# Gathering x2 by source into the tile that uses it, and gathering h2 into a ring of four slots

## What is computed

```python
x = _layernorm(x + _L0(x, edge_attr_48, src, dst, eps))       # relu(x[src] + e) summed by dst
x = _layernorm(x + _L1(x, src, dst, W, b))                    # degree-weighted x[src] summed by dst, @ W
x = _layernorm(x + _L2(x, edge_index, W, b))                  # degree-weighted x[dst] summed by src, @ W
x = _layernorm(x + _L3(x, edge_index, edge_attr_40, ...))     # gated x[dst] summed by src, layernorm, gamma, beta
```

## Time and profile before

| what | value |
|---|---|
| median of the timed runs | 2671.04 us |
| span of the profiled execution | 3047.5 us |
| VectorE busy | 1926.7 us, 63% |
| GpSimd busy | 1858.8 us, 61%, 1768 instructions |
| ScalarE busy | 632.0 us, 21% |
| TensorE busy | 633.7 us, 21% |
| indirect DMAs in `ring`, per gather of 196 | 199.5 to 214.6 us busy |

### The profile page before, as it was taken

One profiled execution on the slowest core, in us unless ns is written; L12 is line 12 of the kernel. 1 busy time (PEld: TensorE's weight loads), 2 busy tenths in 40 slices (PEclk: granted clock), 3 DMA queues, 4 the chain that ended last, 5 costly groups with the idle time before them and its releaser, 6 DMA issues.

```text
span 3047.5 us, 12805 instructions
## 1 busy us (share of the span) xinstructions
PE 633.7 (21%) x2848; PEld 506.5 (17%) x2848; DVE 1926.7 (63%) x2735; ACT 632.0 (21%) x1121; POOL 1858.8 (61%) x1768
## 2 busy tenths in 40 slices
PE   1111600000028875554422100001430000000000
PEld 0000300000028765443422100001330000000000
DVE  2001799999717766754623825997349999948872
ACT  1001800222113332211211101322112223221110
POOL 4774002777766664556175757777556676574776
PEclk8555955555555555666555555555555555555555
DMA  3110086787014433322860193443122223110000
GB/s 118 22 22 13 1 323 231 257 322 269 16 34 142 142 125 103 86 53 55 49 46 13 18 71 114 130 137 119 50 59 72 87 69 103 58 41 9 17 16 15
DMA packets 158467, 276.20 MB, mean 91 GB/s; under 512 B 88601, under 2 KB 113507, under 8 KB 158259
## 3 DMA queue, kind: packets, MB, share of 16 engines
q1 hardware_dynamic: 96675, 206.39, 24.0%
q0 software_dynamic: 56448, 44.23, 8.7%
q10 hardware_dynamic: 5264, 24.74, 2.2%
HBM read 142.41 MB, written 138.17 MB: 92 GB/s over the span
## 4 chain that ended last, share of the span: by engine, by line
DVE 27%; POOL 22%; issue 16%; another core or an unknown queue 12%; PE 8%; DMA 8%; ACT 7%; SPq 0%; ACTq 0%; DVEq 0%; POOLq 0%
POOL XD L470 7%; POOL out L507 7%; POOL x_table L507 3%; POOL ring L457 3%; PE psT L883 2%; DMA din<-x_table 2%; DMA din<-in_xaux 2%; POOL x_with_degree L507 2%; DVE du L1345 2%; DVE var L1351 2%; DVE psS L1342 2%; DVE do L1362 2%; DMA xa_table<-din 2%; DVE sumb L1270 2%
## 5 line engine op out<-in xcount | busy, mean ns | idle before, releaser
L470 POOL DMA_INDIRECT XD<-xa_table,dstI x196 | 222.1, 1133 | 290.5 <-SPq L360 231.0
L507 POOL DMA_INDIRECT x_table<-sumb,put x196 | 212.6, 1085 | 154.7 <-ACT sumb L619 86.5
L457 POOL DMA_INDIRECT ring<-x_with_degree,srcI x196 | 208.2, 1062 | 146.0 <-DVEq L1426 85.1
L592 ACT ACTIVATE sq<-du 128x1344 f32<-128x1344 f32 x129 | 168.9, 1321 | 536.7 <-DVE du L1345 416.5
L457 POOL DMA_INDIRECT ring<-h_by_src,zs x196 | 214.6, 1095 | 104.0 <-issue 63.5
L457 POOL DMA_INDIRECT ring<-x_table,srcI x196 | 199.5, 1018 | 121.1 <-issue 63.2
L507 POOL DMA_INDIRECT x_with_degree<-sumb,put x196 | 209.6, 1070 | 94.0 <-issue 58.1
L507 POOL DMA_INDIRECT out<-sumb,put x196 | 201.9, 1030 | 94.9 <-issue 60.9
L457 POOL DMA_INDIRECT ring<-edge_records,dstI x196 | 202.2, 1032 | 86.8 <-issue 57.6
L470 POOL DMA_INDIRECT XD<-in_xaux,srcI x196 | 187.7, 958 | 87.9 <-issue 60.3
L1240 DVE TENSOR_SCALAR GX<-GX 128x784 bf16<-128x784 int16 x196 | 74.7, 426 | 253.3 <-remote 204.1
(11 more groups left out here) (322 smaller groups left out, 2907.4 us busy)
## 6 DMA issues: line engine op xcount, KB each, us to landing
din<-in_xaux SPq DMA_DIRECT2D x56, 728.0 KB
xa_table<-din SPq DMA_DIRECT2D x28, 728.0 KB
x_table<-GX SPq DMA_DIRECT2D x28, 686.0 KB
x_with_degree<-GX SPq DMA_DIRECT2D x28, 686.0 KB
din<-x_table SPq DMA_DIRECT2D x28, 686.0 KB
x_table<-do SPq DMA_DIRECT2D x28, 672.0 KB
din<-x_table SPq DMA_DIRECT2D x28, 672.0 KB
out<-do SPq DMA_DIRECT2D x28, 672.0 KB
```

Source lines behind the costliest of these rows:

```text
L457: pool.indirect_dma_start(ring[:, h, t, 0:w], None, table, bass.IndirectOffsetOnAxis(ap=of[:, c * H + t:c * H + t + 1], axis=0), **skip).t ...
L470: pool.indirect_dma_start(XD[:, t, 0:w], None, table, bass.IndirectOffsetOnAxis(ap=of[:, t:t + 1], axis=0)).then_inc(rows[c].sem, rows[c]. ...
L507: pool.indirect_dma_start(table, bass.IndirectOffsetOnAxis(ap=put[:, c * H + t:c * H + t + 1], axis=0), rows_of[:, h, t, :], None, bounds_ ...
L592: nc.scalar.activation(sq[:, h, :, :], u, ACT.Square).then_inc(S["squared"], 1)
```

## The change

The x2 gather goes straight to `XD`, column by column, with one semaphore for each turn (`rows_in[c]`), and needs no slot, no copy and no wait. VectorE waits for these semaphores instead of `kept`. The h2 gather uses the memory of `ring` as `ring4`, four slots of 14 x 48 words without gaps (2688 of 2772 words), with a semaphore for each slot's rows and one, `h2_free`, for free slots. ScalarE loads the first two record turns and refills all four slots before the h2 phase, and in the term stage refills the slot that term c has read for turn c + 4.

```diff
+        ring4 = ring[:, :, :, :].rearrange("p h c w -> p (h c w)")[:, 0:4 * H * D].rearrange(
+            "p (h c d) -> p h c d", h=4, d=D)
...
-            def gather_x2(of):
-
-                for c in range(2):
-                    ring_used(c)
-                    gather_turn(X2, D, of, c)
-                gather(X2, D, of, first=2)
+            def gather_h2(of):
+
+                filled, (h2_free,) = views("h2_fill0", "h2_fill1", "h2_fill2", "h2_fill3"), views("h2_free")
+                for c in range(CE // H):
+                    pool.wait_ge(h2_free.sem, h2_free.up())
+                    for t in range(H):
+                        pool.indirect_dma_start(
+                            ring4[:, c % 4, t, :], None, H2,
+                            bass.IndirectOffsetOnAxis(ap=of[:, c * H + t:c * H + t + 1], axis=0),
+                            bounds_check=last_edge, oob_is_err=False
+                                ).then_inc(filled[c % 4].sem, filled[c % 4].add())
...
-            gather_x2(srcI)
+            gather_in_place(X2, D, srcI)
             pool.wait_ge(S["h2_st"], 16 * NBLK)
-            gather(H2, D, put4, bounds_check=last_edge, oob_is_err=False)
+            gather_h2(put4)
...
-            def rows_of_src(c):
-                h = c % 2
-                act.wait_ge(fill[h].sem, fill[h].up(H))
-                nc.scalar.activation(XS[:, c * H:(c + 1) * H, :], ring[:, h, :, 0:D], ACT.Copy
+            def refill(h):
+                nc.scalar.activation(ring4[:, h, :, :], rows[:, 0, :].unsqueeze(1).broadcast_to([P, H, D]), ACT.Copy
                                      ).then_inc(own.sem, own.add())
                 act.wait_ge(own.sem, own.now())
-                if c >= CE // H - 2:
-                    refill(h)
-                act.sem_inc(S["ring_free"], 1)
-                act.sem_inc(S["kept"], 1)
...
-            KEPT_EARLY = {0: (0,), 1: (1,), 3: (2,), 4: (3,), 6: (4,)}
-            KEPT_LATE = {0: (5,), 1: (6,), 2: (7, 8), 3: (9, 10), 4: (11, 12), 5: (13,)}
             h2_rows = H2.rearrange("(p c) d -> p c d", p=P)
+            for h in range(2):
+                act.wait_ge(rb_st[h].sem, rb_st[h].now())
+                load_back(h, h)
+            for h in range(4):
+                refill(h)
+                act.sem_inc(S["h2_free"], 1)
             for i in range(NBLK):
                 evacuate()
                 cols = bass.ds(i * R, R)
                 act.wait_ge(h2_ready.sem, h2_ready.up())
                 act.dma_start(h2_rows[:, cols, :], M[:, cols, :]).then_inc(h2_st.sem, h2_st.add())
-                for c in KEPT_EARLY.get(i, ()):
-                    rows_of_src(c)
-            for h in range(2):
-                act.wait_ge(rb_st[h].sem, rb_st[h].now())
-                load_back(h, h)
...
             def terms_of(c, h, last=False):
                 act.wait_ge(ring_read.sem, ring_read.up())
-                refill(h)
-                act.sem_inc(S["ring_free"], 1)
-                unit = [(h, du[:, h, 0:H, :])]
+                if c + 4 < CE // H:
+                    refill(c % 4)
+                    act.sem_inc(S["h2_free"], 1)
...
-                dve.wait_ge(kept.sem, kept.up(2))
+                for c in (2 * i, 2 * i + 1):
+                    dve.wait_ge(rows_in[c].sem, rows_in[c].up(H))
...
-                dve.wait_ge(fill[h].sem, fill[h].up(H))
-                V.tensor_tensor(u, ring[:, h, :, 0:D], back[:, h, :, 0:D], ALU.add).then_inc(S["ring_read"], 1)
+                dve.wait_ge(filled[c % 4].sem, filled[c % 4].up(H))
+                V.tensor_tensor(u, ring4[:, c % 4, :, :], back[:, h, :, 0:D], ALU.add).then_inc(S["ring_read"], 1)
```

More of the change, by code:

```diff
@@ L251, in bass_gnn @@
             "rec_ready", "rec_st", "srt_ready", "srt_st", "srt_ld",
-            "rb_st0", "rb_st1", "rb_ld0", "rb_ld1", "ring_read", "h2_ready", "h2_st", "by_src", "w1c", "srt_in", "kept",
-            "zt_ready", "zt_st", "z_ld0", "z_ld1", "z_free") + ROWS}
+            "rb_st0", "rb_st1", "rb_ld0", "rb_ld1", "ring_read", "h2_ready", "h2_st", "by_src", "w1c", "srt_in",
+            "zt_ready", "zt_st", "z_ld0", "z_ld1", "z_free", "h2_fill0", "h2_fill1", "h2_fill2", "h2_fill3",
+            "h2_free") + ROWS}
         FROM_DMA = ("look", "g_ld", "g_fill", "g_st", "consts", "edges", "ea48", "xa_ld0", "xa_ld1", "ld0", "ld1",
                     "st0", "st1", "fill0", "fill1", "sc0", "sc1", "mlp_ld0", "mlp_ld1", "mlp_ld2", "mlp_ld3", "rec_st",
-                    "srt_st", "srt_ld", "rb_st0", "rb_st1", "rb_ld0", "rb_ld1", "h2_st", "srt_in", "zt_st", "z_ld0", "z_ld1") + ROWS
+                    "srt_st", "srt_ld", "rb_st0", "rb_st1", "rb_ld0", "rb_ld1", "h2_st", "srt_in", "zt_st", "z_ld0", "z_ld1",
+                    "h2_fill0", "h2_fill1", "h2_fill2", "h2_fill3") + ROWS
         def views(*names):
@@ L772, in _ @@
             function(t0[:, :])
-            def rows_of_src(c):
-                h = c % 2
-                act.wait_ge(fill[h].sem, fill[h].up(H))
-                nc.scalar.activation(XS[:, c * H:(c + 1) * H, :], ring[:, h, :, 0:D], ACT.Copy
-                                     ).then_inc(own.sem, own.add())
-                act.wait_ge(own.sem, own.now())
-                if c >= CE // H - 2:
-                    refill(h)
-                act.sem_inc(S["ring_free"], 1)
-                act.sem_inc(S["kept"], 1)
             def refill(h):
-                nc.scalar.activation(ring[:, h, :, 0:D], rows[:, 0, :].unsqueeze(1).broadcast_to([P, H, D]), ACT.Copy
+                nc.scalar.activation(ring4[:, h, :, :], rows[:, 0, :].unsqueeze(1).broadcast_to([P, H, D]), ACT.Copy
                                      ).then_inc(own.sem, own.add())
@@ L809, in _ @@
                     dense_pair()
-                for c in KEPT_LATE.get(i, ()):
-                    rows_of_src(c)
             act.wait_ge(h2_st.sem, h2_st.now())
@@ L1035, in _ @@
             ld, st, rows_in = views("ld0", "ld1"), views("st0", "st1"), views(*ROWS)
-            squared, std_ready, kept, mm, counted = views("squared", "std_ready", "kept", "mm", "counted")
+            squared, std_ready, mm, counted = views("squared", "std_ready", "mm", "counted")
             mm_used, spread, returned = views("mm_used", "spread", "returned")
@@ L1636, in _ @@
                     dense_pair()
-            rb_ld = views("rb_ld0", "rb_ld1")
+            rb_ld, filled = views("rb_ld0", "rb_ld1"), views("h2_fill0", "h2_fill1", "h2_fill2", "h2_fill3")
             def terms_of(c, h):
@@ L1656, in terms_of @@
                 summed(h, 2)
-            for h in range(2):
-                fill[h].n = 3 * CE // 2 * 16
             term_turn = {own: 8, fill[0]: H, fill[1]: H, spread: 4, ring_read: 2, squared: 2, std_ready: 2,
```

## The result

The changed kernel takes 2631.28 us, the median of 4 runs (2629.29 to 2637.12), beside 2671.36 us for the kernel before (4 runs, 2667.68 to 2671.83): ratio 0.9855, 95% interval 0.9839 to 0.9871, so 40.1 us less. The number of the forecast, 2632, holds. One step of its working does not, and it is the one on which everything else was scaled.

What follows compares the result with a forecast made beforehand. GpSimd's late h2 gather was taken to bound the last terms, once the stalls were put down to profiling. Small edits cost 0, so 2671.0 - 38.7 = 2632.3, forecast 2632 us, range 2622 to 2645.

Steps and rivals of the forecast that it cites:

- the stalls belong to the profiled execution: Whole kernel: 368.7 us of unknown-queue waits exist only in the profiled run; 3047.5 - 368.7 = 2678.8, against 2671.0 timed.
- what bounds the kernel now: Opening step: VectorE bounds the first four term pairs, 49.9 us each; from term 8 GpSimd's 19.84 us turns are late.
- R2: h2 phase: stalls beside a gather are real and grow without pauses, +55 us or twice that, 2687 us; chance 0.07.
- the tail: Last terms, 8 to 13: GpSimd's late h2 rows hold up VectorE; term 13 starts 38.7 us earlier, bounds 36.3 and 40.1.
- part 2: h2 gather: with four ring slots only turns 12 and 13 remain behind the slot term 8 frees, instead of 10 to 13.
- part 1: x2 gather: rows land in XD, removing 57.5 us of ring waits; worth 0 in itself, but h2 gather starts earlier.
- The sum: Term stage end: slot free at 2663.09, two turns and 1.3 us put term 13 at 2705.0 against 2743.67, saving 38.7 us.
- the turn: h2 gather on GpSimd: 14 rows were taken at 20.3 us, up from 19.84, because VectorE no longer pauses beside them.
- (a): ScalarE before the first h2 block: two record loads and four refills take 4.7 us, 2.7 us to spare, cost 0.
- (c): Term stage: record loads back are issued 9.8 us after their term starts; 3 us of slack, so cost 0.
- R1: Term stage: record loads back become the late wait, 1 to 4 us per step, 2634 to 2640 us; chance 0.10.
- R3: Tail stays GpSimd's if the x2 gather ends after 2386, a pitch above 1.44 us a row: 2650 to 2671; chance 0.07.

Runs made afterwards that it cites:

- The 42 rows: Changed kernel with 42 more rows gathered between the x2 and h2 gathers: 2642.95 us, 0.9951 of the kernel before, 26.6 us more than the changed kernel.

## Why the prediction was right, and where it was wrong

**Wrong: the stalls belong to the profiled execution.** This was the first step of "what bounds the kernel now", from two numbers that agree within 8 us. They agree because the profile came from a chip with stalls and the medians from one without, and the change of chip removes just what the chain calls an unknown queue. On chips with stalls the timed runs have them too (3032.42, 3036.05, 3054.99 us). The text also expected the profiled span to grow by R2 while the timed runs shrink: the span fell with the runs, to 2630.5. That the timed runs had no stalls was read correctly from the two numbers, and subtracting the stalls gave a true picture of the other kind of chip: the h2 phase, 141.4 less my 38.9, is 102.5, and was 102.4. But that the comparison fell on a chip without stalls was luck: the working did not know of two kinds of chip, and the case in which the change loses stood in R2 with 0.07.

**R2** was put aside on the same ground, with a chance of 0.07. In the timed comparison it did not decide. On other chips it does, and it was undersized: + 55 us, or twice that, against 181. The price of a block, 33.1 us, was read beside a gather whose pause began 5 us before the block's end (at 2182.5, block in the earlier trace rows); beside an unpaused one the second block is 118 us. The changed kernel itself was not run on such a chip; the variants of three and six slots, which differ from it in the slots alone, say 5 to 6% slower.

**Right: the tail is worth what was said, and it comes from part 2.** The x2 gather was to take 264 us at 1.35 us a row and took 261.9 at 1.34 without a pause; no x2 block waited. On chips with stalls two slots keep the wait of 39 us, four remove it. Neither part was timed alone on a chip without stalls: that part 1 is worth 0 there rests on the term stage, which it leaves at 281 us, and on the x2 blocks, which wait for nothing.

**The sum.** Term 8 to 13 was to be 82.56 - 38.7 = 43.9 us long, and was 42.8. The term of the sum that was off is the turn: 19.83 us, not 20.3; twice 0.5 is the difference. I had let it grow because VectorE no longer pauses beside it. It did not: a row beside the scan takes 1.63 us, as in the earlier trace rows, but the turn keeps its length. The end of the bound at which the Trainium skill ("SBUF — State Buffer", section "SBUF: two separate sides") would have put me, 36.3 us saved, was not reached: the trace shows longer rows beside the scan, as its rule would have them, though no run shows in which mode the scan works; yet 39.8 us were saved.

**Small edits.** (a) ScalarE was to have 2.7 us to spare and had 3.45. (c) The load back lands 4.0 us after its issue, so with an issue 9.8 us behind the start of a term it is there 2.9 us before term c + 2; estimated 3, and R1's cases did not occur:

```profile
GX<-records_by_src ACTq DMA_DIRECT2D x11, 693.0 KB, 4.0
```

**R3** had the start of the h2 gather as the threshold, 19 us away (2367 against 2386). The 42 rows found about 27 us, at 19.4 us a turn unpaused, with the first wait at term 0 and not at the turns that R3 counts.

## What to carry to other kernels

A ring between a producer in bursts and a consumer that slows and then speeds up is sized by what it must store before the consumer's fast stretch: count the turns left behind the last slot that is freed late, and price each at one turn of the producer (here 20 us a slot, up to four). Taking waits off an engine that is not the bound is free only if its pauses served nobody; on some chips the other engines got most of their work in this phase done in them. And when a profile and a median differ by a tenth, ask first whether they are from the same chip.

## What the runs showed of the hardware that was not expected

- Two kinds of chip: beside a stream of indirect DMAs on GpSimd (a row each 1.22 and 1.28 us), TensorE, VectorE and ScalarE start 38 instructions in 50 us on one and 466 on the other. The kernel before takes 3032 to 3055 us on the one and 2657 to 2671 us on the other; the profiles of the one give 11 to 18% of the chain to an unknown queue. TensorE's granted clock in these windows is 0.50 (1.2 GHz) with 19 matmuls and 1.00 (2.4 GHz) with 218. What stalls the engines is not settled; the DMA share, 0.16 in both, does not tell them apart, and GpSimd is even a little faster with stalls.
- Once GpSimd pauses, the others run free: blocks go from 66.8 to 14.6 us. The stalls are uneven. They hit the h2 phase, where TensorE works, but not the x2 blocks behind it: these take 201.2 us beside the gathers with stalls and 201.6 without (1882.52 to 2084.09). The h2 gather beside the terms cost them nothing in seven runs on chips with stalls, and some 10 us a pair in one.
